# Fourier synthesis moved into the prologue of the spiking stage, row block by row block; mixed orders stored through ScalarE's queue

## The chip, the cores and the metric

One Trainium2 (trn2) chip, one core. The metric is the device time of one execution in microseconds. The kernel before has a median of 1368.16 us over three runs (1367.49 to 1375.95). The profile is of one execution that took 1366.96 us.

## What is computed

The input `x` is [8, 32, 64, 128] (batch, H, W, C). Four residual stages follow one another:

```python
x = x + _L0_conv_ref(_ln_c(x), w1r, w1i, w2r, w2i)        # spectral convolution
t = t + _L0_ffn_ref(_ln_t(t))                            # integer shift on one-hot windows of each token
x = x + _L1_conv_ref(_ln_c(x), lin_w, lin_b, bn_*)       # spiking attention over 4 x 8 time steps and heads
t = t + _L1_ffn_ref(_ln_t(t), Wg, bg, W1, b1, W2, b2)    # 8 experts, the 2 best of each token
```

The change lies in the first stage and at the start of the third:

```python
xf    = rfft(x) * (sqrt(2 pi) / NLON)                    # Fourier analysis
x_ft  = einsum('lmj,bcjm->bclm', P_ANA, xf)              # Legendre analysis
top   = einsum('bixy,ioxy->boxy', x_ft[:, :, :M1, :M2], w1)   # mixing with complex weights
bot   = einsum('bixy,ioxy->boxy', x_ft[:, :, -M1:, :M2], w2)
g     = einsum('lmj,bclm->bcjm', P_SYN, out_ft) / sqrt(2 pi)  # Legendre synthesis
out   = irfft(g, n=NLON) * NLON                          # Fourier synthesis, added to x
```

## The kernel before

All of `x` stays in SBUF as `x_sb`: 128 partitions, 128 tiles (batch b by row pair), each with 128 channels and an 8-word payload. The work is laid out in blocks of program (`nc.Block`). In a block each engine runs its own list of instructions in the written order, synchronised by semaphores, and all five engines (SP too) meet at its end before the next one starts. The order within an engine is that of the code. The blocks are:

1. *Analysis* (line 246): SP loads `x` and the Legendre table `pana`, then the first four of eight chunks of mixing weights into the four slots of `wc` (`load_w`, line 211; a chunk is four DMAs of 512 KB). The coefficients go to DRAM.
2. *Mixing* (line 399), eight chunks `n`. ACT loads `coefc`, the coefficients of the chunk; DVE and ACT build `sblk` from it (`blocks`); PE does two halves of 32 matmuls into `ps_m` (line 504); DVE copies the first half to `mo` (`evacuated`, line 436), ACT the second (line 479). `mo` has two slots, so DVE and ACT wait in chunk n for the stores of chunk n - 2 (`s_mw`). On SP, for each chunk: wait for the matmuls of chunk n, load the weights of chunk n + 4, wait for both halves of `mo`, store them to the DRAM tensor `mixed` by two DMAs (lines 402 to 411).
3. *Synthesis* (line 545). SP loads the tables `psyn` (2 MB) and `einv`, reads `mixed` back as `gin` by 16 DMAs, and fills the DRAM tensor `slots` with zero rows by four DMAs of 2652 KB (line 559); no other engine waits for those here. PE does 32 Legendre matmuls into two banks `ps_g` (line 573), and ACT and DVE take turns to empty them into `h_sb` (line 542), laid out batch by batch. Then for each of the eight batches: POOL copies the batch to `hc` (line 627), PE turns eight tiles (line 586), ACT copies them to `hT` (line 616), PE multiplies them by `einv` into `ps_y` (line 594), and DVE adds the result to `x_sb` (line 642).
4. *Weights* of the spiking stage (line 678): SP loads `lw` and five parameter vectors `par`. DVE, with one POOL instruction, scales them (`bpart`, line 711), PE does eight transposes (lines 721, 723), and DVE makes `wqkv`, `bias` and `wo`.
5. *Opcodes and spikes* (line 1320). Its *prologue* prepares row block 0 (two tiles of each batch): `statistics` (line 874) on DVE, `deviation` on POOL, `u_rows` and `x_rows` (lines 1232, 1242) on ACT, `ffn_flags`, `ffn_value`, `ffn_shift`, `ffn_add` and `z_statistics` on DVE, `deviation_2` on POOL, `z_rows` (line 1252) on ACT, `turn` (line 1130) on PE, `major` (line 1262) on ACT. Then nine passes `i` over eight steps `b` follow: each step begins with `project` (PE), `sign_projected` (ACT, the tile `sig_q`), `projected` (DVE), and the functions `beside` and `behind` say what else stands in a step. SP loads constants and, in 14 DMAs, the expert weights into `routing.raw` and `routing.last` (lines 1333 to 1344).
6. *Experts* (line 1621), 156 tiles, bound by PE.

The wait that limits a step of the grid in stage 3, and the wait that stands at the end of the store's loop on SP:

```python
pe.wait_ge(s_hT, b * 2 + g + 3)      # grid(g): turned tiles copied by ACT
pe.wait_ge(s_yfree, b * 2 + g + 1)   # grid(g): bank added by DVE
for k in range(2):
    sp.wait_ge(s_mw[k], STORED * NCH // 2)
```

## Time and profile before

| what | value |
|---|---|
| runs, median (range) | 1368.16 us (1367.49 to 1375.95) |
| profiled execution, its own time | 1366.96 us |
| its span, first to last instruction | 1364.5 us |
| mean granted clock of TensorE | 0.835 |
| busy: PE, PEld, DVE, ACT, POOL | 993.5, 845.5, 857.8, 655.1, 573.4 us |
| mixing, from the first matmul to the next block | 104.67 to 203.19 |
| synthesis | 203.19 to 283.73 |
| weights, and prologue up to the first sign | 283.73 to 345.76 |
| moved by DMA | 93.08 MB |

PE is TensorE's matmuls, PEld its weight loads, DVE VectorE, ACT ScalarE, POOL GpSimd, SP the engine that only issues DMAs. "L504" is line 504 of the kernel before. In a timeline row the number behind the start is the length, from the first to the last of the instructions merged in it; the bracket says how long the engine stood idle before it and what ended that. For SP the length is the time that issuing took. The span's idle shares are means over stages that are limited by different things, so times are read stage by stage.

### The profile page before, as it was taken

What the parts mean: (1) busy time and instruction counts of PE and PEld (TensorE: products, weight loads), DVE (VectorE), ACT (ScalarE), POOL (GpSimd) and SP (SyncE); (2) the same over time, 40 slices, a digit from 0 to 9 for tenths busy, and PEclk for the clock granted to TensorE, in tenths of its full rate; (3) what the DMA queues carried; (4) which work ended last, traced back from release to release, by engine and by line L of the source; (5) the groups of instructions that cost most, each with busy time, mean ns of one, the idle gap of its engine ahead of it and who ended that gap; (6) DMA issues with size and microseconds to landing.
All of it is one profiled execution on the core that took longest, in us unless ns stands there. A gap on an engine that the chain in (4) does not pass through costs nothing. (4 is left out here: it accounts for less than half of the span.)

```text
span 1364.5 us, 23969 instructions
## 1 busy us (share of the span) xinstructions
PE 993.5 (73%) x6628; PEld 845.5 (62%) x6629; DVE 857.8 (63%) x2741; ACT 655.1 (48%) x1400; POOL 573.4 (42%) x739
## 2 busy tenths in 40 slices
PE   7937665931577767676776754129999999999997
PEld 6827663721355556565565543028888888888886
DVE  6715432454557889889878454616666666666675
ACT  3427532207385887777865342114444444444443
POOL 3310000212022257566655477645555555555554
PEclk9978887875777888797867655559999999999999
DMA  9998949910001001000000000011111111111110
GB/s 277 201 236 157 210 104 261 240 43 20 19 20 49 20 19 41 15 24 23 11 26 15 28 25 27 21 51 45 42 43 46 48 48 48 45 47 48 46 37 1
DMA packets 122841, 93.08 MB, mean 68 GB/s; under 512 B 10760, under 2 KB 111476, under 8 KB 122001
## 3 DMA queue, kind: packets, MB, share of 16 engines
q1 hardware_dynamic: 103121, 66.48, 21.6%
q0 software_dynamic: 9088, 17.33, 3.9%
q10 hardware_dynamic: 10560, 8.39, 2.3%
q8 instruction: 35, 0.57, 0.2%
q14 instruction: 37, 0.30, 0.1%
HBM read 55.61 MB, written 38.39 MB: 69 GB/s over the span
## 5 line engine op out<-in xcount | busy, mean ns | idle before, releaser
L1663 POOL DMA_INDIRECT out_dram<-res,index x156 | 155.8, 999 | 217.7 <-DVE res L1746 192.4
L1793 ACT ACTIVATE sil<-ps_h 128x512 f32<-128x512 f32 x156 | 93.1, 597 | 254.6 <-PE ps_h L1845 254.6
L1711 DVE TENSOR_TENSOR act_rows<-ps_h,sil 128x512 f32<-128x512 f32 x156 | 108.0, 692 | 132.9 <-ACT sil L1793 132.8
L1864 PE MATMUL ps_y<-r_raw,aT 128*128 x1248 | 164.9, 275 | 0.0
L153 POOL DMA_INDIRECT slots<-x_sb,r_pos x128 | 130.9, 1023 | 54.0 <-issue 33.0
L1864 PEld LDWEIGHTS ps_y<-r_raw,aT 128*128 128x128 f32 x1248 | 151.7, 192 | 0.1
L1843 PE MATMUL ps_h<-wp,uTh 128*128 x312 | 137.5, 441 | 1.9 <-DVE uTl L1705 1.6
L1844 PE MATMUL ps_h<-wp,uTh 128*128 x312 | 124.4, 399 | 0.0
L1845 PE MATMUL ps_h<-wp,uTl 128*128 x312 | 122.8, 394 | 0.0
L1070 PE MATMUL ps_q<-wqkv,zT 128*128 128x256 f32 x256 | 114.5, 540 | 0.0
L1182 POOL TENSOR_TENSOR x_sb<-x_sb,sy 128x256 f32<-128x256 f32 x64 | 43.9, 687 | 145.6 <-ACT sy L1318 145.4
L1070 PE MATMUL ps_q<-zT,wqkv 128*128 128x128 f32 x256 | 72.6, 377 | 42.4 <-DVE ps_q L1038 24.0
L504 PE MATMUL ps_m<-wc,sblk 128*128 128x128 f32 x512 | 68.8, 304 | 39.9 <-DVE mo L442 22.6
L1296 ACT ACTIVATE sig_q<-ps_q,under_one 128x768 bf16<-128x768 f32 x64 | 57.4, 897 | 82.2 <-PE ps_q L1070 82.2
L1070 PEld LDWEIGHTS ps_q<-zT,wqkv 128*128 128x128 f32 x256 | 54.6, 264 | 63.6 <-ACT zT L1266 23.2
L1853 PE MATMUL ps_a<-ident,act_rows 128*128 128x128 f32 x624 | 93.5, 272 | 0.1
L504 PEld LDWEIGHTS ps_m<-wc,sblk 128*128 128x128 f32 x512 | 67.8, 220 | 41.1 <-issue 41.1
L1799 ACT ACTIVATE aT<-ps_a 128x512 f32<-128x512 f32 x156 | 92.4, 592 | 1.0 <-PE ps_a L1853 1.0
L1853 PEld LDWEIGHTS ps_a<-ident,act_rows 128*128 128x128 f32 x624 | 77.5, 140 | 21.7 <-DVE act_rows L1711 0.6
L194 POOL TENSOR_TENSOR e_tmp<-e_tmp,minus_half 128x16 f32<-128x16 f32 x16 | 46.8, 2924 | 91.3 <-DVE e_tmp L178 91.2
L1038 DVE SCALAR_TENSOR_TENSOR ps_q<-sig_q,ps_q 128x768 f32<-128x768 bf16 x56 | 54.6, 974 | 48.6 <-ACT sig_q L1296 48.4
L627 POOL COPY hc<-h_sb 128x1024 f32 x8 | 8.3, 1040 | 163.0 <-DVE h_sb L542 140.5
(233 smaller groups left out, 2482.8 us busy)
## 6 DMA issues: line engine op xcount, KB each, us to landing
slots<-zero SPq DMA_DIRECT2D x4, 2652.0 KB, 26.2
pay<-slots SPq DMA_DIRECT2D x39, 272.0 KB, 2.8
wc<-in_L_conv_w1r SPq DMA_DIRECT2D x8, 512.0 KB, 11.4
wc<-in_L_conv_w1i SPq DMA_DIRECT2D x8, 512.0 KB, 11.8
wc<-in_L_conv_w2r SPq DMA_DIRECT2D x8, 512.0 KB, 11.7
wc<-in_L_conv_w2i SPq DMA_DIRECT2D x8, 512.0 KB, 11.7
coefficients<-c ACTq DMA_DIRECT2D x4, 1024.0 KB, 8.6
coefc<-coefficients ACTq DMA_DIRECT2D x16, 256.0 KB, 6.1
```

The lines of the kernel that those rows point to most:

```text
L153: nc.gpsimd.indirect_dma_start(slots, bass.IndirectOffsetOnAxis(at, 0), x_sb[:, tile, :], None).then_inc(self.s_sc, 16)
L504: ins = nc.tensor.matmul(ps_m[:, half, t, :], sblk[:, n % 2, l, m:m + 4].rearrange("p m f -> p (m f)"), wc[:, n % WS, :, l, m:m + 4], star ...
L1070: return nc.tensor.matmul(out, lhs, rhs, start=first, stop=True, skip_group_check=True)
L1663: nc.gpsimd.indirect_dma_start(out_rows, bass.IndirectOffsetOnAxis(at, 0), res[:, m % RES, :], None, bounds_check=TOKENS - 1, oob_is_err=F ...
L1711: nc.vector.tensor_tensor(act_rows[:, k], ps_h[:, k, :, DFF:], sil[:, k], ALU.mult).then_inc(s_act, 1)
L1793: nc.scalar.activation(sil[:, k], ps_h[:, k, :, 0:DFF], ACT.Silu).then_inc(s_sil, 1)
L1799: nc.scalar.activation(aT[:, k, :], ps_a[:, :], ACT.Copy).then_inc(s_ac, 1)
L1843: nc.tensor.matmul(dst, hi, wp[:, 0, :, col], start=True, stop=False)
L1844: nc.tensor.matmul(dst, hi, wp[:, 1, :, col], start=False, stop=False)
L1845: ins = nc.tensor.matmul(dst, lo, wp[:, 0, :, col], start=False, stop=True)
L1853: ins = nc.tensor.transpose(ps_a[:, h * P:(h + 1) * P], act_rows[:, k, h // 2, (h % 2) * P:(h % 2 + 1) * P], ident[:, :])
L1864: ins = nc.tensor.matmul(dst, aT[:, k, (2 * e + h) * P:(2 * e + h + 1) * P], raw[:, 4 + h, col], start=(h == 0), stop=(h == 1))
```

## The change

It has three parts.

*Stores.* In the mixing block the two stores of `mixed` go from SP's list to ACT's, behind ACT's half of the same chunk. SP keeps only the weight loads. Every chunk is still loaded, multiplied and stored as before.

*Blocks.* The synthesis block is dissolved. Its loads, Legendre part and zero fills join the weights in one block (`synthesis_and_weights`): on SP the weights' six loads stand between `psyn` and `einv`; on PE and DVE the weights' work stands ahead of the Legendre part. The orders `h_sb` now lie in the space of the expert weights (`routing.orders`), so the loads of `routing.raw` wait until all of them are turned.

*Grid.* The Fourier synthesis goes by row block `i` (two row pairs of all batches) instead of by batch, in the prologue of the next block: `orders_turned` and `grid` on PE, `orders_copied` on ACT, `grid_added` on DVE. POOL's copy `hc` goes, since the transposes read the orders in place. The accumulators are the two banks `ps_o` and `ps_y` in turn (two matmuls each), and the turned tiles go through `ps_kv`. PE does all eight row blocks ahead of its first `turn`; DVE and ACT have them between the steps of the prologue. `u_rows` and `x_rows` of row block 1 move from before the first sign to steps 0 to 3 of the first pass, and `major(0, 0)` stands ahead of `z_rows` 1 to 3.

In what follows the rows of each engine's list are printed for three places. On ACT, at the last chunk of the mixing; `mo` is the tile of mixed orders. Before:

```order
L485 ACTIVATE mo<-ps_m 32x2x256 [waits mixed_stored_0,m_mixed]
L485 ACTIVATE mo<-ps_m 32x2x256 x3
L485 ACTIVATE mo<-ps_m 32x2x256 [waits mixed_stored_1,m_mixed]
L485 ACTIVATE mo<-ps_m 32x2x256 x3
L399 UNCONDITIONAL_BRANCH
```

The same place now:

```order
L481 ACTIVATE mo<-ps_m 32x2x256 [waits mixed_stored_0,m_mixed]
L481 ACTIVATE mo<-ps_m 32x2x256 x3
L497 DMA mixed<-mo 128x4x128 [waits m_last_degrees_out,m_first_degrees_out]
L497 DMA mixed<-mo 128x4x128
L481 ACTIVATE mo<-ps_m 32x2x256 [waits mixed_stored_1,m_mixed]
L481 ACTIVATE mo<-ps_m 32x2x256 x3
L497 DMA mixed<-mo 128x4x128 [waits m_last_degrees_out,m_first_degrees_out]
L497 DMA mixed<-mo 128x4x128
```

The stores have come to ACT, and each waits for both halves of its chunk.

On SP, from the start of the synthesis to the end of the block. Before:

```order
L548 DMA psyn<-in_legendre_synthesis 128x4096
L549 DMA einv<-in_fourier_inverse 128x256
L555 DMA gin<-mixed 32x2048 x16
L559 DMA slots<-zero 128x39x136 [waits e_zero]
L559 DMA slots<-zero 128x39x136 x3
L545 UNCONDITIONAL_BRANCH
L679 UNCONDITIONAL_BRANCH [waits barrier_Pool_Activation_PE_DVE_SP_release]
L681 DMA lw<-in_L_conv_lin_w 128x4x128
```

Now:

```order
L572 DMA psyn<-in_legendre_synthesis 128x4096
L573 DMA lw<-in_L_conv_lin_w 128x4x128
L576 DMA par<-in_L_conv_lin_b 128x4x1
L576 DMA par<-in_L_conv_bn_g 128x4x1
L576 DMA par<-in_L_conv_bn_b 128x4x1
L576 DMA par<-in_L_conv_bn_m 128x4x1
L576 DMA par<-in_L_conv_bn_v 128x4x1
L577 DMA einv<-in_fourier_inverse 128x256
L583 DMA gin<-mixed 32x2048 x16
L587 DMA slots<-zero 128x39x136 [waits e_zero]
L587 DMA slots<-zero 128x39x136 x3
L569 UNCONDITIONAL_BRANCH
```

The block's end has come directly behind the zero fills, and the six weight loads ahead of `gin`.

On DVE, at the start of the prologue; `e_st` holds the statistics. Before:

```order
L184 BN_STATS e_st<-x_sb 128x6 x16
L172 TENSOR_TENSOR e_tmp<-e_st 128x16 [waits e_statistics_chain]
...
L1360 CAST before<-before_f 128x128 [waits e_constants]
L885 TENSOR_SCALAR fl<-u 128x16 [waits e_ffn_rows,r_constants_set]
```

Now:

```order
L839 TENSOR_TENSOR x_sb<-x_sb,ps_o 128x2x2x128 [waits c_grid]
L839 TENSOR_TENSOR x_sb<-x_sb,ps_y 128x2x2x128 [waits c_grid]
L839 TENSOR_TENSOR x_sb<-x_sb,ps_o 128x2x2x128 [waits c_grid]
L839 TENSOR_TENSOR x_sb<-x_sb,ps_y 128x2x2x128 [waits c_grid]
L185 BN_STATS e_st<-x_sb 128x6 [waits c_added]
L185 BN_STATS e_st<-x_sb 128x6 x15
...
L839 TENSOR_TENSOR x_sb<-x_sb,ps_o 128x2x2x128 [waits c_grid]
L839 TENSOR_TENSOR x_sb<-x_sb,ps_y 128x2x2x128 [waits c_grid]
L839 TENSOR_TENSOR x_sb<-x_sb,ps_o 128x2x2x128 [waits c_grid]
L839 TENSOR_TENSOR x_sb<-x_sb,ps_y 128x2x2x128 [waits c_grid]
```

Four adds of a row block now stand ahead of the statistics, and four behind them.

The diff, cut to its core (the synthesis block that goes is in the functions printed above):

```diff
-        spectral_conv(nc, t, sb, pb, sem, x_sb, ident, minus_half, x_view, slots, routing)
+        mixed = spectral_conv(nc, t, sb, pb, sem, x_sb, ident, minus_half, x_view, routing)
...
-            weights = spiking_weights(nc, t, sb, pb, sem, ident, minus_half, a, routing)
+            weights = synthesis_and_weights(nc, t, sb, pb, sem, ident, minus_half, a, mixed, slots, routing)
...
-        self.raw = sb("r_raw", [P, 6, E * C])
+        kept = sb("r_raw", [P, 10, E * C])
+        self.raw, self.last = kept[:, 0:6], kept[0:C - 1, 6:10]
+        self.orders = kept[:, 0:8].rearrange("p a f -> p (a f)").rearrange("p (b h r m) -> p b h r m", b=B, h=HP, r=2)
...
                     for n in range(NCH):
-                        k = n % 2
                         if n + WS < NCH:
                             sp.wait_ge(s_mm, n + 1)
                             load_w(sp, n + WS)
-                        sp.wait_ge(s_ed, n + 1)
-                        sp.wait_ge(s_ea, n + 1)
-                        for op in range(2):
-                            sp.dma_start(mixed[op, n * LQ:(n + 1) * LQ].rearrange("l p f -> p l f"),
-                                         mo[:, k, op].rearrange("p (l m) o -> p l (m o)", l=LQ)).then_inc(s_mw[k], 16)
...
                         evacuated(n)
+                        act.wait_ge(s_ed, n + 1)
+                        act.wait_ge(s_ea, n + 1)
+                        for op in range(2):
+                            act.dma_start(mixed[op, n * LQ:(n + 1) * LQ].rearrange("l p f -> p l f"),
+                                         mo[:, n % 2, op].rearrange("p (l m) o -> p l (m o)", l=LQ)).then_inc(s_mw[n % 2], 16)
...
+        def grid_bank(u):
+            return (ps_o if u % 2 == 0 else ps_y)[:, :]
+
+        def orders_turned(pe, i, g):
+
+            need(pe, s_chT, (i - 1) * 2 + g + 1)
+            for q in range(G):
+                ins = nc.tensor.transpose(ps_kv[:, g, q * P:(q + 1) * P],
+                                          h_sb[:, g * G + q, 2 * i:2 * i + 2].rearrange("p h r m -> p (h r m)"), ident[:, :])
+            ins.then_inc(s_ct, 1)
+
+        def orders_copied(act, i, g):
+
+            act.wait_ge(s_ct, i * 2 + g + 1)
+            need(act, s_cg, ((i - 1) * 2 + g) * 2 + 2)
+            nc.scalar.activation(hT[:, g, :], ps_kv[:, g, :], ACT.Copy).then_inc(s_chT, 1)
+
+        def grid(pe, i, g):
+
+            pe.wait_ge(s_chT, i * 2 + g + 1)
+            for h in range(2):
+                u = (i * 2 + g) * 2 + h
+                need(pe, s_ca, u - 1)
+                for q in range(2):
+                    at = (h * 2 + q) * P
+                    ins = nc.tensor.matmul(grid_bank(u)[:, q * 2 * C:(q + 1) * 2 * C], hT[:, g, at:at + P], einv[:, :],
+                                           start=True, stop=True)
+                ins.then_inc(s_cg, 1)
+
+        def grid_added(dve, i):
+
+            for n in range(4):
+                u = i * 4 + n
+                dve.wait_ge(s_cg, u + 1)
+                rows = xv[:, 2 * n:2 * n + 2, i]
+                nc.vector.tensor_tensor(rows, rows, grid_bank(u).rearrange("p (b j c) -> p b j c", b=2, j=2), ALU.add).then_inc(s_ca, 1)
...
+                sp.wait_ge(s_ct, 2 * NP2)
                 for k in range(4):
                     sp.dma_start(routing.raw[0:C - 1, k, :].rearrange("p (e f) -> p e f", e=E),
...
+                grid_added(dve, 0)
                 statistics(dve, 0)
+                grid_added(dve, 1)
...
+                grid_added(dve, 2)
+                grid_added(dve, 3)
                 ffn_flags(dve, 0)
+                grid_added(dve, 4)
                 ffn_value(dve, 0)
                 ffn_shift(dve, 0)
+                grid_added(dve, 5)
+                grid_added(dve, 6)
                 ffn_add(dve, 0)
                 z_statistics(dve, 0)
+                grid_added(dve, 7)
                 statistics(dve, 1)
...
-                u_rows(act, 0, 0, NT)
-                x_rows(act, 0, 0, NT)
-                for g in range(G):
+                for i in range(3):
+                    copied(i)
+                u_rows(act, 0, 0, 8)
+                copied(3)
+                u_rows(act, 0, 8, NT)
+                copied(4)
+                x_rows(act, 0, 0, 5)
+                copied(5)
+                x_rows(act, 0, 5, 10)
+                copied(6)
+                x_rows(act, 0, 10, NT)
+                copied(7)
+                z_rows(act, 0, 0)
+                major(act, 0, 0)
+                for g in range(1, G):
                     z_rows(act, 0, g)
-                major(act, 0, 0)
-                u_rows(act, 1, 0, NT)
-                x_rows(act, 1, 0, NT)
...
-                    if b == 0 and 2 <= n < NP2:
+                    if b == 0 and n < NP2:
                         u_rows(act, n, 0, 10)
...
+                pe.wait_ge(s_einv, 16)
+                for i in range(NP2):
+                    for g in range(2):
+                        orders_turned(pe, i, g)
+                    for g in range(2):
+                        grid(pe, i, g)
                 pe.wait_ge(s_set, 1)
                 turn(pe, 0, 0)
...
+                        if k == 0:
+                            pe.wait_ge(s_ca, 4 * NP2)
                         if k >= 0:
                             attend(pe, i - 1, b)
```

## Rows read from the trace of the kernel before

**Rows 1.** Windows by stage: length, busy us (instructions) by engine, granted clock, DMA share, GB/s.
```profile
104.67:203.19 98.52, 68.76 (x512) 67.75 (x512) 45.38 (x110) 56.37 (x116) 0.00 (x0) 0.85 0.83 161
203.19:283.73 80.54, 57.95 (x256) 46.29 (x256) 28.77 (x40) 17.07 (x24) 8.26 (x8) 0.84 0.90 215
283.73:345.76 62.03, 7.28 (x28) 5.06 (x28) 25.99 (x144) 29.43 (x81) 11.26 (x11) 0.55 0.16 36
```

**Rows 2.** Timeline of SP's queue, weight loads: start, length, line, tile, count.
```profile
43.66 2.61 SPq L214 DMA_DIRECT2D wc<-in_L_conv_w1r  x1
...
55.32 2.71 SPq L214 DMA_DIRECT2D wc<-in_L_conv_w1r  x1
...
114.39 0.56 SPq L214 DMA_DIRECT2D wc<-in_L_conv_w1r  x1
```

**Rows 3.** Windows of 4 us, columns as in rows 1.
```profile
104.00:108.00 4.00, 3.33 (x15) 3.36 (x16) 2.44 (x9) 3.04 (x8) 0.00 (x0) 0.50 0.53 129
...
172.00:176.00 4.00, 3.40 (x31) 3.21 (x29) 0.00 (x0) 0.00 (x0) 0.00 (x0) 1.00 1.17 232
176.00:180.00 4.00, 0.00 (x0) 0.00 (x0) 2.32 (x4) 2.05 (x4) 0.00 (x0) 0.72 0.44 132
...
192.00:196.00 4.00, 4.00 (x39) 4.00 (x38) 2.47 (x4) 0.30 (x1) 0.00 (x0) 1.00 0.43 133
...
264.00:268.00 4.00, 4.00 (x23) 3.41 (x21) 1.89 (x3) 0.24 (x1) 0.36 (x1) 1.00 1.06 244
...
284.00:288.00 4.00, 0.00 (x0) 0.00 (x0) 0.00 (x0) 0.00 (x0) 0.00 (x0) 0.88 0.52 68
```

**Rows 4.** Waits in 100 to 204: us in total, times, longest.
```profile
DVE mo L442 <- DMA mixed<-mo: 32.8, 4, 10.6
```

**Rows 5.** Timeline of PE in the mixing: start, length, tile, count, idle before.
```profile
166.39 9.01 PE L504 MATMUL ps_m<-wc,sblk 128*128 128x128 f32 x64 [4.07 <-DVE mo L442]
180.58 16.45 PE L504 MATMUL ps_m<-wc,sblk 128*128 128x128 f32 x128 [5.18 <-DVE mo L442]
```

**Rows 6.** Timeline of all engines, synthesis and weights.
```profile
203.19 0.34 SPq L548 DMA_DIRECT2D psyn<-in_legendre_synthesis  x1
...
212.07 44.23 SPq L559 DMA_DIRECT2D slots<-zero  x4
...
217.28 6.10 PE L573 MATMUL ps_g<-gin,psyn 128*128 128x256 f32 x16 [20.25 <-DMA gin<-mixed]
...
239.75 1.97 PE L586 MATMUL ps_t<-ident,hc 128*128 128x128 f32 x8 [2.64 <-POOL hc L627]
...
247.35 1.04 PE L586 MATMUL ps_t<-ident,hc 128*128 128x128 f32 x8
...
252.27 1.04 PE L586 MATMUL ps_t<-ident,hc 128*128 128x128 f32 x8
...
288.81 0.27 DVE L695 MEMSET bias<- 128x256 uint32 x1 [5.36 <-DMA par<-in_L_conv_bn_v]
...
294.62 1.11 PE L721 MATMUL ps_w<-ident,lw 128*128 128x128 f32 x4 [12.65 <-DVE bpart L711]
```

**Rows 7.** SP's own waits in 90 to 300: total, times, longest.
```profile
SPq L545 <- PEq L545: 27.2, 1, 27.2
```

**Rows 8.** Timeline of all engines, prologue.
```profile
299.18 3.19 DVE L184 BATCH_NORM_STATS2 e_st<-x_sb 128x6 f32<-128x128 f32 x16 [0.30 <-PEq L678]
...
303.56 2.90 POOL L194 TENSOR_TENSOR e_tmp<-e_tmp,minus_half 128x16 f32<-128x16 f32 x1 [4.31 <-DVE e_tmp L178]
...
312.42 0.17 DVE L885 TENSOR_SCALAR fl<-u 128x16 f32<-128x16 f32 x1 [7.87 <-ACT u L1237]
...
318.71 1.02 DVE L934 SCALAR_TENSOR_TENSOR x_sb<-eq,x_sb 128x128 f32<-128x128 f32 x4 [0.60 <-ACT x_sb L1247]
...
327.75 6.26 ACT L1258 ACTIVATE z<-x_sb,e_tmp 128x128 f32<-128x128 f32 x16 [9.14 <-POOL e_tmp L1225]
...
345.76 0.88 ACT L1296 ACTIVATE sig_q<-ps_q,under_one 128x768 bf16<-128x768 f32 x1
```

188 lines of the change are left out of this document (64 added, 124 removed).

## The prediction

> **What bounds the kernel now.** I read the stages first: the windows [rows 1] give mixing 98.5 us, synthesis 80.5 us, weights and prologue 62.0 us. The change touches these three and the first pass of the loop behind them. No engine fills any of them: TensorE (PE) is busy 68.8, 58.0 and 7.3 us. They are three chains, one behind the other, so the question is which wait ends last in each.
>
> In mixing a weight chunk (four 512 KB loads) on its own takes 11.7 us: such chunks are issued at 43.66 and 55.32. Chunk 4 is issued at 114.39 [rows 2]. At 172 to 176 the DMA engines are still full (share 1.17), and in the next 4 us the share falls to 0.44. A 0.5 MB `mixed` store alone takes 0.43 of 4 us, 1.7 us, and a 0.5 MB `coefc` load 0.53 of 4, 2.1 us [rows 3]. Chunks 4 to 7, four coefficient loads and five stores are 46.6 + 8.4 + 8.6 = 63.6 us, and 114.4 + 63.6 = 178.0, in the window where the share falls: the sum closes, so the stretch is bound by bytes. But VectorE (DVE) also stood 32.8 us in four waits for stores to land [rows 4], since the stores are behind the weight loads on SP. So when the bytes are through, two chunks of matmuls are still to do: PE runs both (16.45 us) from 180.58 to 197.0 [rows 5]. ScalarE (ACT) empties the last bank, and the next block starts at 203.19 [rows 6].
>
> In synthesis the `gin` loads give PE its first work 14.1 us after the block starts (217.28). The Legendre part ends at about 238.2 (PE stands 2.64 us before the first turn at 239.75, the last copy of about 1 us among it); then come eight batches, the first in 7.6 us, the others in 4.92 us each (247.35 to 252.27). Beside it SP needs until 256.3 to issue four zero fills (44.23 us) [rows 6]; DMA is full until nearly 268 [rows 3]. SP then waits 27.2 us for PE: a block ends for all engines together [rows 7]. Weights then take 15.4 us, and the prologue 46.6 us from 299.18 to the first sign at 345.76 [rows 6, 8].
>
> **The change, part by part.** Times are in the profiled execution (1366.96 us, span 1364.5).
>
> *Mixing.* Stores no longer queue behind the weight loads, and DVE's waits fall away. What is late next is the last weight chunk. Before it must land: 46.6 us of weights, 8.4 of coefficients and, now that stores keep up, six stores, 10.3: 114.4 + 65.3 = 179.7. PE has finished chunk 6 by then (its weights land some 12 us earlier), so one chunk remains instead of two. PE has stood before it: a chunk after such a wait took 9.01 us, the second of two in a row 16.45 - 9.0 = 7.4 [rows 5] (in 172 to 176 the granted clock was 1.00, 2.4 GHz, and 0.72 in the next 4 us, part at 1.2 GHz, when PE stood). It ends at 189 where it ended at 197.0: **-8 us**. On ACT the store waits for DVE's half of the same chunk, which is done before ACT's, and blocks nothing. Bounds: 0 if two streams in the engines cost what the order saves; -16 if the stores cost nothing and the last chunk is fast. I take -8, from the sum that closed.
>
> The row at 172 says full engines, whatever the order of issue. The Trainium skill, "DMA: Bandwidth & Descriptors", section "Issuing engines are not separate DMA queues", says that starting DMAs from several engines saves only the sequencer's issue time, since all share the same 16 engines. By that rule the sum would be 8 us higher; DVE's 32.8 us of waits speak for an effect of the order, so I keep it as a rival below.
>
> *Synthesis block with the weights in it.* Count from its start. The weights' six loads (0.52 of 4 us, 2.1 us [rows 3]) come behind the 2 MB table and ahead of `gin`. My estimate for their landing is 10: 5.1 us as before (283.73, idle until 288.81) and 5 more for the table. From there to the end of PE's eight transposes is 7.8 us (288.81 to 294.62 and two groups of 1 us [rows 6]), so PE is free at 17.8 and Legendre starts there, not at 14.1. It takes 20.9 us and ends at 38.7. The weights' 15.4 us are hidden by loads. But the block cannot end there: SP issued its last fill 53.1 us after the block start (212.07 + 44.23 - 203.19), and now has 2.1 us more of data ahead, so it ends at 55.5. The fills' old cover, the grid, has left the block, and 16.8 us of the gain are lost. Before, block and weights took 299.18 - 203.19 = 96.0: **-40.5 us**. Bounds: 38.7 if SP does not hold the others, 60 if fills and weights disturb each other.
>
> *Prologue with the grid in it.* The same transposes and wide matmuls come in eight rows of 4.92 us; POOL's `hc` copies go. With the slow first row that is 39.4 + 2.7 = 42.1 us. The accumulators are two banks in turn, so PE runs at most two halves (1.9 us) ahead of DVE, and what DVE does between adds holds PE. Statistics take 4.3 us (299.18 to 303.5) and hold row 1 by 2.9, as the add before them has to be done first. Flags, value and shift take 5.7 us (312.42 until 0.60 us before 318.71 [rows 8]); flags, over half, hold row 4 by 1.6, the rest row 5 by 0.9. Row 6 ends at 2.7 + 7 x 4.92 + 5.4 = 42.5. DVE adds it (0.8; its mean instruction in [rows 1] is 0.72), does `ffn_add` (1.1) and the second statistics (4.2): 48.6. ACT's `u` and `x` rows (each at most the 6.26 us of the 16 `z` rows) lie between its copies, under the grid. Then the old chain: POOL 3.5 (2.90 and two small ones), first four `z` rows 1.6, turn, copy and gaps 1.6, and twelve `z` rows 4.7 that stand ahead of the first sign: **60 us** for 46.6 before, **+13.4 us**. The last PE row waits for DVE until 48.6 too and ends at 51, under this chain. Constants queue behind what is left of the fills (268 - 256.3 = 11.7 us), land at about 12, and are wanted at 17: hidden; uncovered they would cost a few us. Bounds: 54 (no holds) to 86 (grid, then the prologue with little overlap).
>
> *First pass of the loop.* `u_rows` and `x_rows` of row block 1, at most 12.5 us of ACT, stood before the first sign and now lie behind signs 0 to 3, in four portions of 3 us and less, where ACT waits for PE and DVE in turn: +1 us, bounds 0 to +6. What took them away is in the 60. The raw weight loads start about 11 us earlier in the span, and nobody waits for them until the experts: 0. The `s_ca` wait before the first attention is met long before: 0.
>
> Sum: -8 - 40.5 + 13.4 + 1 = -34.1, and 1366.96 - 34.1 = 1332.9. The median of the runs is 1.2 us over the profiled one, which gives 1334. I say **1333.5 us**, -2.5%.
>
> **The rivals.**
> 1. *SP does not hold the block.* 16.8 us more are gained: 1317. For it: no engine is seen waiting for SP at a block's end. Against: SP waited 27.2 us for PE at the same line.
> 2. *The store move gives nothing*: 1341.5. For it: full DMA engines. Against: DVE's 32.8 us, and two chunks left at the end.
> 3. *The grid does not overlap the prologue*, 86 us instead of 60: 1359.5, within 1%. For it: PE, ACT and DVE wait for each other in each row. Against: in four of eight rows nothing but adds stands on DVE.
> 4. *The fills become the bound and the kernel is slower.* Place: the end of the synthesis block. If fills, `gin` and weights' small loads in one ring crawl, SP's 44 us of issue grow and every engine waits. From 34 us more there is no gain, from 48 us more (92 us of issue, half the rate) it is slower by over 1%, 1382. Against: even the fills' last window shows 244 GB/s and a share of 1.06 [rows 3], and nothing ahead of them is large but the table and `gin`, as before.
>
> **How the numbers follow.** The forecast has 0.62 (its own range 1326 to 1342), rival 1 0.13, rival 2 0.12, rival 3 0.10, rival 4 0.03. The range 1314 to 1347 holds the first three and leaves out rivals 3 and 4 and the outer bounds of the others, about 0.2. A measurement of this kernel can tell about 1% from no change: below 1354.5 are the forecast, rivals 1 and 2 and the half of rival 3 with part of the overlap, 0.91; within 1% 0.06; slower 0.03.
>
> **What would show it.** Right: PE waiting for the last weights before chunk 7 and the next block at about 195; the last fill's issue ending last in the block at about 250.5, the others waiting for SP; PE waiting for DVE's adds in rows 1, 4, 5 and 7; the first `sig_q` at about 311. Wrong: a block that ends before SP's last fill (rival 1), a next block at 203 (rival 2), a first sign beyond 330 (rival 3), or passes of the loop longer than before.

## The result, and the profile after

The changed kernel takes 1331.38 us in the median of five runs (1325.47 to 1350.04). The kernel before, in the same series, has 1368.16 us (1367.40 to 1383.62). The ratio is 0.974, with a 95% interval of 0.969 to 0.979: 2.6% faster. The forecast was 1333.5 us, within 1314 to 1347. The total came out about 2 us off, but the terms of the sum were off in opposite directions: mixing gained more than forecast, the other three stages less. The stages show that, not the total.

The execution whose profile came with this result was disturbed in the analysis stage, which no edit touches (the last section is about that), so the rows below are from a second profile of the same kernel, `after_again`, with a span of 1324.6 us. I cut both profiles at the same events: first mixing matmul, first DMA of the next block (`psyn`), first DMA of the block behind it (`rank`), first sign (`sig_q`), ninth sign. The table has those differences, and forecast ones beside them:

| us | before | forecast | after_again | measured change |
|---|---|---|---|---|
| until the first mixing matmul | 104.7 | 104.7 | 104.8 | +0.1 |
| mixing | 98.5 | 90.5 | 81.6 | -16.9 |
| synthesis and weights | 95.9 | 55.5 | 56.8 | -39.1 |
| prologue | 46.6 | 60 | 62.4 | +15.8 |
| first pass, eight signs | 43.2 | 44.2 | 46.4 | +3.2 |
| rest of the span | 975.5 | 975.5 | 972.6 | -2.9 |

**Windows.** These are the three stages of the changed kernel, with the columns of [rows 1]: stretch, length, busy us and instructions of PE, PEld, DVE, ACT and POOL, granted clock, DMA share, GB/s.

```profile
104.80:186.36 81.56, 64.06 (x512) 62.87 (x512) 45.39 (x110) 56.41 (x116) 0.00 (x0) 0.92 0.91 194
186.36:243.16 56.80, 20.18 (x72) 13.43 (x73) 14.54 (x39) 8.36 (x8) 1.03 (x2) 0.68 1.07 251
243.16:305.56 62.40, 50.19 (x212) 38.85 (x212) 40.65 (x145) 26.87 (x66) 9.06 (x8) 0.83 0.32 78
```

The first row answers to the first of [rows 1]. PE does the same 512 matmuls, and the DMA engines move the same bytes at 194 GB/s instead of 161. The second row shows the block as it is now: PE has 20 us of work in 57, and DMA is full (1.07). The grid has gone to the third row, where PE is now busy 50 of 62 us.

**Mixing.** The timeline of PE, for all of the stage: start, length, line, tile, count, and in brackets what ended the idle time before.

```profile
104.80 16.66 PE L505 MATMUL ps_m<-wc,sblk 128*128 128x128 f32 x128 [16.41 <-ACT sblk L472]
123.57 7.38 PE L505 MATMUL ps_m<-wc,sblk 128*128 128x128 f32 x64 [2.11 <-ACT sblk L472]
...
163.61 7.38 PE L505 MATMUL ps_m<-wc,sblk 128*128 128x128 f32 x64 [1.11 <-ACT sblk L472]
172.76 7.41 PE L505 MATMUL ps_m<-wc,sblk 128*128 128x128 f32 x64 [1.76 <-DMA wc<-in_L_conv_w2i]
```

In place of the two chunks at the end of [rows 5] (x128, behind a wait for DVE's `mo`) there is one, and it waits for the last weight load. DVE's 32.8 us of waits for stores [rows 4] are gone. The form is as forecast; the times are not. The last weights were forecast 75.0 us after the first mixing matmul (179.7), and the chunk at 9.0 us. It starts 68.0 us after it and takes 7.4. The other waits of PE in the stage are for ACT's `sblk`: ACT's list comes round every 10.0 us per chunk (its copies to `mo` start at 124.31, 134.28, 144.27 and 154.23), so ACT now sets the pace nearly as tightly as the weights do.

**Block.** The timeline of all engines in the block. SPq rows are DMA issues.

```profile
186.36 0.35 SPq L572 DMA_DIRECT2D psyn<-in_legendre_synthesis  x1
...
189.63 5.40 SPq L576 DMA_DIRECT2D par<-in_L_conv_bn_m  x1
...
196.19 7.68 SPq L583 DMA_DIRECT2D gin<-mixed  x16
197.51 0.27 DVE L599 MEMSET bias<- 128x256 uint32 x1 [18.09 <-DMA par<-in_L_conv_bn_v]
...
203.31 1.12 PE L634 MATMUL ps_w<-ident,lw 128*128 128x128 f32 x4 [23.14 <-DVE bpart L615]
203.91 38.82 SPq L587 DMA_DIRECT2D slots<-zero  x4
...
205.07 4.33 PE L645 MATMUL ps_g<-gin,psyn 128*128 128x256 f32 x12
...
224.30 1.01 DVE L566 COPY r_raw<-ps_g 128x512 f32<-128x512 f32 x1 [1.22 <-PE ps_g L645]
...
243.17 1.94 PE L811 MATMUL ps_kv<-ident,r_raw 128*128 128x128 f32 x8 [18.91 <-PEq L569]
```

The parameters have landed at 197.51, 11.1 us into the block (forecast 10), and Legendre starts 18.7 us into it (forecast 17.8). The last Legendre copy (the orders now lie in the space called `r_raw`) ends at 225.3. SP issues zero fills until 242.7. PE then does its first turn, after 18.91 us without anything of its own to wait for: `PEq L569` is the block's own line, its end. This answers to SP's wait of 27.2 us in [rows 7], with the roles exchanged.

**Prologue.** The timeline of PE at the start of the rows that it had to wait for DVE, and the one of ACT at the end:

```profile
256.56 2.05 PE L829 MATMUL ps_o<-einv,hT 128*128 128x256 f32 x4 [2.68 <-DVE x_sb L839]
...
274.79 1.10 PE L829 MATMUL ps_o<-einv,hT 128*128 128x256 f32 x4 [1.47 <-DVE x_sb L839]
...
280.81 1.10 PE L829 MATMUL ps_o<-einv,hT 128*128 128x256 f32 x4 [0.94 <-DVE x_sb L839]
...
294.60 2.04 PE L829 MATMUL ps_o<-einv,hT 128*128 128x256 f32 x4 [3.61 <-DVE x_sb L839]
...
297.52 1.65 ACT L1226 ACTIVATE z<-x_sb,e_tmp 128x128 f32<-128x128 f32 x4 [8.09 <-POOL e_tmp L1193]
300.92 4.71 ACT L1226 ACTIVATE z<-x_sb,e_tmp 128x128 f32<-128x128 f32 x12
305.54 0.88 ACT L1264 ACTIVATE sig_q<-ps_q,under_one 128x768 bf16<-128x768 f32 x1
```

They are rows 1, 4, 5 and 7 of the eight, counted from 0, and no others.

### The profile page after: what moved, and what is told of

Same layout as the page of the kernel before. It is cut to its first block and busy times, and to the rows that moved or that the text cites. A ratio compares the mean times of both kernels' runs of the same rounds, so it can differ in the third digit from the quotient of the medians.

```text
span 1348.2 us, 23795 instructions
## 1 busy us (share of the span) xinstructions
PE 1019.1 (76%) x6628; PEld 869.1 (64%) x6629; DVE 859.9 (64%) x2741; ACT 656.3 (49%) x1400; POOL 565.4 (42%) x731
## 5 line engine op out<-in xcount | busy, mean ns | idle before, releaser
L1662 POOL DMA_INDIRECT out_dram<-res,index x156 | 156.0, 1000 | 217.2 <-DVE res L1745 186.2
L505 PE MATMUL ps_m<-wc,sblk 128*128 128x128 f32 x512 | 63.5, 289 | 29.5 <-ACT sblk L472 27.7
L505 PEld LDWEIGHTS ps_m<-wc,sblk 128*128 128x128 f32 x512 | 62.3, 204 | 30.9 <-issue 28.8
L1038 PE MATMUL ps_o<-spk,kvm 128*128 128x64 bf16 x256 | 20.8, 211 | 77.9 <-DVE ps_o L1025 76.9
## 6 DMA issues: line engine op xcount, KB each, us to landing
wc<-in_L_conv_w1i SPq DMA_DIRECT2D x8, 512.0 KB, 12.7
wc<-in_L_conv_w2i SPq DMA_DIRECT2D x8, 512.0 KB, 11.9
```

Source lines behind the costliest of these rows:

```text
L505: ins = nc.tensor.matmul(ps_m[:, half, t, :], sblk[:, n % 2, l, m:m + 4].rearrange("p m f -> p (m f)"), wc[:, n % WS, :, l, m:m + 4], star ...
L1038: return nc.tensor.matmul(out, lhs, rhs, start=first, stop=True, skip_group_check=True)
L1662: nc.gpsimd.indirect_dma_start(out_rows, bass.IndirectOffsetOnAxis(at, 0), res[:, m % RES, :], None, bounds_check=TOKENS - 1, oob_is_err=F ...
```

## The experiments

Eleven runs were made, one of them the changed kernel again. Each was profiled once and timed against the kernel before on the same chip. Ratios are to the kernel before, with their 95% interval. Their totals scatter by some 1% with the analysis stage (after_again's six executions took 1324.62 to 1347.21 us), so a verdict on a stage goes by the stage's own length, cut as above:

| us | mixing | Legendre end | block | prologue | first pass | rest | span |
|---|---|---|---|---|---|---|---|
| before | 98.5 | 35.0 | 95.9 | 46.6 | 43.2 | 975.5 | 1364.5 |
| after | 82.8 | 37.9 | 56.6 | 60.1 | 46.5 | 976.5 | 1348.2 |
| after_again | 81.6 | 38.9 | 56.8 | 62.4 | 46.4 | 972.6 | 1324.6 |
| stores_sp | 97.5 | 39.2 | 57.5 | 60.4 | 45.7 | 968.2 | 1344.7 |
| stores_twice | 95.0 | 38.7 | 57.0 | 60.4 | 47.2 | 975.5 | 1361.1 |
| before_stores_act | 81.4 | 34.8 | 95.0 | 46.6 | 43.7 | 974.7 | 1354.6 |
| fills_later | 83.2 | 38.2 | 38.5 | 60.0 | 45.4 | 972.1 | 1325.5 |
| four_banks | 83.7 | 38.1 | 56.2 | 54.9 | 46.8 | 976.8 | 1321.3 |
| z_behind | 81.3 | 38.5 | 56.3 | 62.9 | 53.0 | 972.2 | 1351.2 |
| u_first | 82.6 | 38.0 | 56.7 | 72.8 | 43.2 | 973.5 | 1354.6 |
| best_a | 81.4 | 38.7 | 39.0 | 52.9 | 46.8 | 972.2 | 1305.6 |
| best_b | 81.4 | 35.2 | 35.4 | 52.9 | 46.7 | 970.0 | 1291.0 |
| weights_two | 86.9 | 38.1 | 56.3 | 60.0 | 46.5 | 973.5 | 1334.6 |

"Legendre end" is the last copy out of `ps_g`, counted from the block's start; "block" in the two kernels built as before is synthesis and weights together. What a span has over the sum of its stages is the time until the first mixing matmul, 102.9 to 126.3 us. A stage that no edit touches keeps its length within 1 to 2.5 us from kernel to kernel (the rest of the span, some 970 us, within 9), and that is what a difference has to exceed. Only best_a and best_b have totals whose intervals do not overlap that of after_again, so the other experiments speak through their stages.

### The mixing: whose 16 us?

**after_again**, the changed kernel once more, as the other end of each comparison.

> The changed kernel once more, since its profiled execution was a disturbed one: it spent 125.7 us before the first mixing matmul, where the kernel before spent 104.7. If that was the execution and not the change, the first mixing matmul is back at about 105 and the span about 21 us shorter than 1348, near 1328. If the change slows the analysis stage, it stays at 125. Mixing (first matmul to next block) 82.8 us, synthesis block 56.6, prologue to first sign 60.1 as in the first profile, all within 1 us.

Measured: 1338.62 us in the median, ratio 0.976 [0.967, 0.985]. The interval overlaps that of the first series. The first mixing matmul is back at 104.8 and the span is 1324.6, so the analysis stage was the execution's and not the change's. Mixing (81.6) and prologue (62.4) missed "all within 1 us" by a little: the first is 1.2 us shorter than in the first profile, the second 2.3 longer.

**stores_sp**: the changed kernel with the stores back on SP's list.

```diff
                         if n + WS < NCH:
                             sp.wait_ge(s_mm, n + 1)
                             load_w(sp, n + WS)
+                        sp.wait_ge(s_ed, n + 1)
+                        sp.wait_ge(s_ea, n + 1)
+                        for op in range(2):
+                            sp.dma_start(mixed[op, n * LQ:(n + 1) * LQ].rearrange("l p f -> p l f"),
+                                         mo[:, n % 2, op].rearrange("p (l m) o -> p l (m o)", l=LQ)).then_inc(s_mw[n % 2], 16)
...
-                        act.wait_ge(s_ed, n + 1)
-                        act.wait_ge(s_ea, n + 1)
-                        for op in range(2):
-                            act.dma_start(mixed[op, n * LQ:(n + 1) * LQ].rearrange("l p f -> p l f"),
-                                         mo[:, n % 2, op].rearrange("p (l m) o -> p l (m o)", l=LQ)).then_inc(s_mw[n % 2], 16)
```

> The changed kernel with only the stores of mixed orders put back on SP's queue. Theory A (the forecast: bytes bind, the order saves one chunk of matmuls): mixing 8 us longer than in the changed kernel, about 91. Theory B (stores and weight loads in two queues overlap in the DMA engines, more than one queue allows): the whole 15.7 us come back, mixing 98.5, time about 1345. Rival 2 (the store move gives nothing): no difference, 83.

Measured: 1352.45 us, ratio 0.989 [0.979, 0.998]. Mixing is 97.5 us, all of the old length but 1 us, and the other stages stay. The waits of the trace show the old row again (engine, line, what it waited for, total, times, longest):

```profile
DVE mo L443 <- DMA mixed<-mo: 32.5, 4, 10.6
```

**before_stores_act**: the same move, alone, in the kernel before. The diff is that of stores_sp read backwards, on the kernel before.

> The kernel before with only the stores moved to ScalarE's queue, the rest as it was. Forecast: 8 us faster, about 1360. Theory B: 15.7 us faster, about 1352, and mixing 82.8 as in the changed kernel. Rival 2: no difference, 1368.

Measured: 1354.97 us, ratio 0.988 [0.979, 0.997]. Mixing is 81.4 us, -17.1. So the store move is worth 16 to 17 us with or without the rest of the change, and the parts of the change do not interact here.

**stores_twice**: the changed kernel, with each chunk stored a second time, to a DRAM tensor that nobody reads.

```diff
-            STORED = 16 * 2
+            STORED = 16 * 4
...
+                        for op in range(2):
+                            act.dma_start(twice[op, n * LQ:(n + 1) * LQ].rearrange("l p f -> p l f"),
+                                         mo[:, n % 2, op].rearrange("p (l m) o -> p l (m o)", l=LQ)).then_inc(s_mw[n % 2], 16)
```

> The changed kernel with every store of mixed orders issued a second time, into a DRAM tensor that nobody reads; the output is unchanged. Theory A (bytes of all queues add up at 1.7 us for a 0.5 MB store): six more stores ahead of the last weight chunk make mixing 10 us longer, about 93. Theory B (stores in a queue of their own fill gaps of the weight loads): under 4 us longer, with more GB/s in the saturated stretch than the 237 of the changed kernel.

Measured: 1354.96 us, ratio 0.988 [0.977, 0.999]. Mixing is 95.0 us, 13.4 more than in after_again. The number is theory A's, but the trace shows another cause: the weights were not late. PE starts chunk 7 at 205.62, 70.2 us after SP issued chunk 4's weights at 135.41 (58.4 us in after_again), and what it waits for is ACT:

```profile
205.62 7.38 PE L510 MATMUL ps_m<-wc,sblk 128*128 128x128 f32 x64 [1.45 <-ACT sblk L474]
```

The last weights had landed by 194.1. This table has, for each kernel, the stretch from the first load of chunk 4 to the landing of the last load of chunk 7, and what all queues moved in it:

| | issued | landed | us | MB | DMA share | GB/s |
|---|---|---|---|---|---|---|
| before | 114.39 | 176.1 | 61.7 | 12.7 | 1.15 | 205 |
| stores_sp | 124.62 | 186.2 | 61.6 | 12.8 | 1.15 | 207 |
| after_again | 114.34 | 172.7 | 58.4 | 13.6 | 1.13 | 234 |
| before_stores_act | 122.28 | 180.9 | 58.6 | 13.7 | 1.14 | 234 |
| stores_twice | 135.41 | 194.1 | 58.7 | 15.2 | 1.13 | 258 |

With 4.6 MB of stores beside them instead of 3.1, the weights took 0.3 us longer. What the doubled stores cost is time on ACT, which issues them between its copies and the next `sblk`. These are ACT's waits with nothing but its own issues in them, first in stores_twice, then in after_again:

```profile
ACT sblk L472 <- issue: 18.8, 6, 4.0
ACT sblk L470 <- issue: 6.9, 6, 1.3
```

They differ by 11.9 us, and chunk 7 starts 11.8 us later. So theory B is right about the transfers and wrong about the stage, whose length ACT's list sets here: its round takes up to 12.9 us per chunk instead of 10.

The rate of the saturated stretch shows in windows of 15 us. The kernel before (columns as above):

```profile
120.00:135.00 15.00, 8.89 (x78) 8.54 (x76) 6.76 (x18) 12.15 (x26) 0.00 (x0) 0.95 1.18 212
135.00:150.00 15.00, 9.54 (x64) 9.38 (x64) 4.30 (x14) 5.67 (x14) 0.00 (x0) 0.83 1.16 215
150.00:165.00 15.00, 9.53 (x64) 9.37 (x64) 7.71 (x19) 9.09 (x19) 0.00 (x0) 0.77 1.18 208
```

And the same stretch of after_again, whose mixing begins within 0.2 us of it:

```profile
120.00:135.00 15.00, 10.31 (x85) 9.98 (x84) 9.14 (x25) 11.69 (x26) 0.00 (x0) 0.94 1.17 238
135.00:150.00 15.00, 13.86 (x117) 13.70 (x117) 10.69 (x26) 11.55 (x24) 0.00 (x0) 0.95 1.16 247
150.00:165.00 15.00, 11.29 (x84) 10.96 (x84) 8.82 (x25) 12.50 (x27) 0.00 (x0) 0.89 1.16 246
```

The share is the same, 1.16 to 1.18, in both: by it the engines were full before, and are full now. The last column rose from 212 to 244 GB/s, and the table has 258 in stores_twice. A full share is not a full rate, and that is what the forecast's byte sum took it for.

**weights_two**: of each chunk's four loads from the fifth chunk on, two are issued by SP and two by GpSimd (POOL), with a semaphore of their own. It asks whether more queues for the loads gain more.

```diff
-                            load_w(sp, n + WS)
+                            load_w(sp, n + WS, range(2))
...
                     nc.gpsimd.memset(sblk[:, 1], 0.0).then_inc(s_zero, 1)
+                    for n in range(NCH - WS):
+                        pool.wait_ge(s_mm, n + 1)
+                        load_w(pool, n + WS, range(2, 4), s_p)
...
-                        pe.wait_ge(s_w[n % WS], n // WS * 64 + 64)
+                        pe.wait_ge(s_w[n % WS], n // WS * 32 + 64)
+                        need(pe, s_p[n % WS], n // WS * 32)
```

> The changed kernel, but of each mixing chunk's weights from the fifth on two of the four transfers are issued by GpSimd and two by SP; bytes and waits are the same. It asks where the mixing stage's missing 8 us went (forecast 90.5, measured 81.6 to 82.8). If more queues at once fill gaps that one queue leaves in the engines (loads alone ran at 181 to 185 GB/s, loads with stores on another queue at 232 to 256), a third queue fills more of them: mixing 72 to 78, GB/s of the stretch above 240 from the fifth chunk's issue on. If the 16 us came from SP no longer issuing stores ahead of loads (order within the queue, not number of queues), two queues for the loads change nothing: mixing 81 to 83. If GpSimd's own queue costs more per transfer, it is longer: 85 or more.

Measured: 1335.55 us, ratio 0.973 [0.966, 0.980], and mixing of 86.9 us, 4 to 5 longer. The first two expectations missed. The third has the number right, but not the cause. PE's timeline at the end, and DVE's waits in the stage:

```profile
163.44 7.38 PE L509 MATMUL ps_m<-wc,sblk 128*128 128x128 f32 x64 [0.75 <-ACT sblk L476]
174.62 17.43 PE L509 MATMUL ps_m<-wc,sblk 128*128 128x128 f32 x128 [3.79 <-DVE mo L442]
```

```profile
DVE mo L442 <- DMA mixed<-mo: 18.2, 3, 8.6
```

PE waits for no weights. It could not gain much by them either: in the changed kernel only 1.76 us of its waits in this stage were for weights, and ACT's list takes 10.0 us per chunk, so mixing of 72 to 78 us was out of reach of any rate of the loads. The stores land later (10.0 us after their issue in the median, 18.4 at most; 8.2 and 10.0 in after_again), DVE waits for them again, and as in the kernel before, two chunks are left at the end. Here the third queue for the loads took service from the stores, and what came late decided, not the rate alone.

### The block: is it held by SP?

**fills_later**: the four zero fills go to the next block, behind its constants.

```diff
-                sp.wait_ge(routing.s_zero, 2)
-                part = SLOT_TILES // 4
-                for n in range(4):
-                    sp.dma_start(slots.rearrange("(q p) c -> p q c", p=P)[:, n * part:(n + 1) * part, :],
-                                 routing.zero[:, :].unsqueeze(1).broadcast_to([P, part, XW])).then_inc(routing.s_clear, 16)
...
+                sp.wait_ge(routing.s_zero, 2)
+                part = SLOT_TILES // 4
+                for n in range(4):
+                    sp.dma_start(slots.rearrange("(q p) c -> p q c", p=P)[:, n * part:(n + 1) * part, :],
+                                 routing.zero[:, :].unsqueeze(1).broadcast_to([P, part, XW])).then_inc(routing.s_clear, 16)
                 sp.wait_ge(s_ct, 2 * NP2)
```

> The changed kernel with only the four zero fills moved on SP from the end of the synthesis block to the next block, behind the constants and ahead of the expert weights. Theory of the forecast (the block ends when SP has issued its last fill): the block ends with the Legendre part at about 38.5 us instead of 56.6, time 18 us less, about 1311. Rival 1 (SP does not hold the others, something else fills the gap from 246 to 265): the block stays at 56 us and the time at 1329. A third way: the fills now run beside the grid and cost it something, gain 10 to 15.

Measured: 1324.76 us, ratio 0.965 [0.957, 0.973]. The block is 38.5 us, 18.3 shorter than in after_again, and ends 0.3 us behind the last Legendre copy. PE's row of waits:

```profile
PE ps_kv L806 <- PEq L569: 1.4, 1, 1.4
```

It was 18.91 us. The fills are issued within the prologue, and that stays at 60.0 us. The total missed the 1311 us of the expectation: the profiled execution stood 126.3 us in the analysis stage, 21 more than after_again. Rival 1 of the forecast (SP does not hold the block) is refuted by both kernels: one shows engines standing for SP's issue, the other what it costs.

### The prologue

**four_banks**: the grid's accumulators go round four PSUM banks instead of two, so PE may run four halves ahead of DVE's adds.

```diff
-            return (ps_o if u % 2 == 0 else ps_y)[:, :]
+            return (ps_o[:, :], ps_y[:, :], ps_q[:, 0], ps_q[:, 1])[u % 4]
...
-                need(pe, s_ca, u - 1)
+                need(pe, s_ca, u - 3)
...
+            if k == 0:
+                pe.wait_ge(s_ca, 4 * NP2)
```

> The changed kernel with the grid's accumulators in four banks in turn (the two banks of ps_q join ps_o and ps_y) instead of two. Forecast's theory (PE is held in rows 1, 4 and 5 by 5.4 us in sum, because DVE does other work between adds and PE is only two halves ahead): prologue 5 us shorter, first sign at 55 us from the block's start instead of 60.1, waits of PE for DVE's adds in those rows gone. Rival (DVE's own chain is the limit, PE only waits beside it): prologue stays within 1 us of 60.

Measured: 1325.28 us, ratio 0.974 [0.966, 0.982], prologue 54.9 us, 5.2 less than in the first profile of the changed kernel and 7.5 less than in the second. PE's waits for DVE's adds are gone from the trace. So the three holds inside the grid, 2.9 + 1.6 + 0.9 = 5.4 us in the forecast and 2.7 + 1.5 + 0.9 = 5.1 in the trace, stood on the path in full. The 2.3 us by which the two profiles of the changed kernel differ are no part of that.

**u_first**: `u_rows` and `x_rows` of row block 1 stand before the first sign again, where the kernel before has them.

```diff
                 for g in range(1, G):
                     z_rows(act, 0, g)
+                u_rows(act, 1, 0, NT)
+                x_rows(act, 1, 0, NT)
...
-                    if b == 0 and n < NP2:
+                    if b == 0 and 2 <= n < NP2:
```

(and the same condition for b = 1 to 3)

> The changed kernel with u_rows and x_rows of row block 1 put back ahead of the first sign, as in the kernel before. Forecast's term (their place in steps 0 to 3 costs 1 us, ahead of the sign they would cost 11.5 less what the first projection hides): 8 to 11 us slower than the changed kernel, first sign at 71, first pass 43.2 us again instead of 46.5. If their place makes no difference: within 1 us.

Measured: 1354.83 us, ratio 0.984 [0.974, 0.994]. The prologue is 72.8 us, 10.4 longer than in after_again and 12.7 longer than in after, and the first pass is 43.2 us, exactly as before. The rows cost 11.45 us where they stand in front:

```profile
326.50 5.19 ACT L1205 ACTIVATE u<-x_sb,e_tmp 128x48 f32<-128x48 f32 x16 [1.20 <-POOL e_tmp L1184]
331.73 6.26 ACT L1215 ACTIVATE x_sb<-x_sb,e_tmp 128x128 f32<-128x128 f32 x16
337.89 0.88 ACT L1264 ACTIVATE sig_q<-ps_q,under_one 128x768 bf16<-128x768 f32 x1
```

and 3.2 us in the steps of the first pass. That is the answer to the term of +1 for this edit.

**z_behind**, a miss: twelve of the sixteen `z` rows go behind the first three signs, in the hope of a first sign 4.7 us earlier.

```diff
-                for g in range(1, G):
-                    z_rows(act, 0, g)
...
+                        if i == 0 and b < 3:
+                            z_rows(act, 0, b + 1)
```

> The changed kernel with the twelve z rows of groups 1 to 3 moved from ahead of the first sign to behind signs 0, 1 and 2 of the first pass. If ScalarE's 4.7 us stand on the path to the first sign: first sign 2 to 3 us earlier (it then waits for PE's projection), and the first pass up to 3 us longer since ScalarE is full there too: gain 0 to 3 us. If ScalarE has room in those steps the gain stays at 3.

Measured: 1347.08 us, ratio 0.982 [0.974, 0.991]. The prologue does not get shorter (62.9 us), and the first pass is 53.0 us, 6.6 longer. PE turns each group of `z` for a step still ahead, and now waits for it (rows of PE's timeline, one for each of the three groups that were moved):

```profile
328.42 1.12 PE L1105 MATMUL ps_turn<-ident,z 128*128 128x128 f32 x4 [2.52 <-ACT z L1226]
335.72 1.12 PE L1105 MATMUL ps_turn<-ident,z 128*128 128x128 f32 x4 [2.77 <-ACT z L1226]
343.43 0.66 PE L1105 MATMUL ps_turn<-ident,z 128*128 128x128 f32 x4 [3.18 <-ACT z L1226]
```

The first sign needs PE's projection, and that was on its way while ACT did the twelve rows. With the rows gone, ACT stands idle for most of their 4.71 us:

```profile
325.94 0.90 ACT L1264 ACTIVATE sig_q<-ps_q,under_one 128x768 bf16<-128x768 f32 x1 [3.87 <-PE ps_q L1038]
```

Where they stood they cost less than 1 us.

### A version that beats both

**best_a** is fills_later and four_banks together, with no further edit.

> The changed kernel with the two edits that paid by their stages put together: zero fills issued in the next block, behind its constants, and the first grid's accumulators in four PSUM banks. If the two gains are independent, the stages add up: mixing 81.6, block 38.5 (fills out of it), prologue 55 (from 60.1 to 62.4), first pass 46 to 47, rest unchanged; that is 18 + 5 to 7 us below the changed kernel's own stages, a total near 1310 us (ratio 0.957 to the kernel before). The rival: with the fills in the prologue, SP's queue and the 16 engines are busy until about 33 us after the block's start, and the rows that now leave two PSUM banks earlier meet the fills; then the prologue stays at 58 to 60 and the total at 1316.

Measured: 1307.41 us, ratio 0.950 [0.939, 0.961]. Block 39.0, prologue 52.9 us. The gains add up, and the rival (the fills in the prologue meet the faster rows) is refuted: the prologue is 2 us shorter than in four_banks, which is within what it varies by, and not longer than there.

**best_b** is best_a with the weights' six loads moved to the end of the mixing block, into tiles of their own.

```diff
+        self.lw = sb("lw", [P, 4, C])
+        self.par = sb("par", [P, 5, 4])
...
                             load_w(sp, n + WS)
+                    sp.dma_start(routing.lw[:, :, :], t["L1_conv_lin_w"].rearrange("i d c -> d i c")).then_inc(routing.s_load, 16)
+                    for n, name in enumerate(("lin_b", "bn_g", "bn_b", "bn_m", "bn_v")):
+                        with nc.allow_non_contiguous_dma(reason="512 parameters, once"):
+                            sp.dma_start(routing.par[:, n, :], t[f"L1_conv_{name}"].rearrange("i d -> d i")).then_inc(routing.s_load, 16)
...
-        lw = sb("lw", [P, 4, C], at=a)
-        par = sb("par", [P, 5, 4], at=a)
+        lw, par = routing.lw, routing.par
```

> best_a, and the longitude block's Linear weights and its five parameter vectors are loaded at the end of the mixing stage's load queue, into tiles of their own. If the 5 to 6 us by which the Legendre stage's end is later in the changed kernel than its own PE work asks (the five vectors' transfers, 5 us each in the queue, ahead of the grid's input) are the cause, the Legendre stage ends 35 us or less after the block's start instead of 38 to 39, and the block is 3 to 5 us shorter: 34 to 35.5. The rival: the vectors' small packets are only waited for elsewhere (in the mixing stage, behind the last chunk's weights), then mixing grows by what the block loses, 3 to 5 us, and the total stays that of best_a.

Measured: 1297.06 us, ratio 0.946 [0.938, 0.954]. The interval overlaps that of best_a, so the totals alone do not tell the two apart; the stage does. Legendre ends at 35.2 us and the block at 35.4, 3.6 less than in best_a, and mixing is unchanged at 81.4. The expectation had 5 us of queue for each of the five vectors; in the changed kernel one issue took 5.40 us and the others 0.50 to 1.06. What was late is no longer the parameters but `gin` (waits of PE and DVE in the block; the first row is DVE waiting for the mixing block to end):

```profile
DVE bias L596 <- PEq L403: 7.1, 1, 7.1
PE ps_g L642 <- DMA gin<-mixed: 6.7, 1, 6.7
```

The three stages in windows:

```profile
104.40:185.84 81.44, 64.19 (x512) 63.06 (x512) 45.42 (x111) 56.40 (x116) 0.00 (x0) 0.92 0.89 197
185.84:221.29 35.45, 20.40 (x72) 13.68 (x72) 14.59 (x39) 8.31 (x8) 1.01 (x1) 0.73 0.71 182
221.29:274.17 52.88, 42.02 (x212) 34.75 (x212) 39.70 (x145) 26.57 (x65) 10.26 (x10) 0.94 0.99 232
```

The fills' DMA work has moved to the third row (share 0.99, where after_again has 0.32), beside a PE that is busy four fifths of the time, and the prologue is no longer for it (52.9 us, 54.9 in four_banks). These three stages take 169.8 us, where the changed kernel has 200.8 and the kernel before 241.1. The mixing holds a second test of its pace: the last weights landed 54.8 us after chunk 4's issue, 3.6 sooner than in after_again, and the stage did not get shorter, since PE waited for ACT's `sblk` instead (1.60 us before chunk 7).

## Why the prediction was right or wrong

**Mixing, -8: mis-sized, it is -16.9.** The mechanism was right: the stores' place on SP was the cause, DVE's waits went, and one chunk is left at the end instead of two. The step that failed is "before it must land: 46.6 us of weights, 8.4 of coefficients and six stores, 10.3". The sum of 65.3 us took the share of 1.17 for the limit of the engines and added loads and stores as if one had to wait for the other. It measured 58.4 us, 7 less. About 2 us of that were wrong before the change: the sum closed at 178.0, but the weights had landed at 176.1, 61.7 us after the issue, and the SP queue had moved 2.1 MB of stores by then, which is four chunks and not five. Another 1.7 are the sixth store, which cost the loads nothing, and 3.3 are the higher rate with the stores in ACT's queue. The remaining 1.6 us are the last chunk itself, 7.4 us instead of 9.0: PE had stood only 1.76 us before it, and the granted clock of 165 to 180 is 1.00, of the 15 us before it 0.89. The far bound of -16 was given for just these two things, stores that cost nothing and a fast last chunk; the measured value is just beyond it. Had the weights landed as late as in the kernel before, 71.4 us after the first matmul and not 67.9, the stage would be 3.5 us longer. So by this estimate most of the gain, some 13 us, is the order in SP's list, as forecast but larger, and some 3.5 us are the second queue. What the forecast did not see at all is that ACT, with its 10.0 us per chunk, is as long as the weights now: in best_b they came 3.6 us sooner for nothing. I had one hint and did not weigh it: the sum closed for one queue, and I then used it for two. Rival 2, the store move gives nothing, rested on the same rows, and it is refuted by stores_sp and before_stores_act. The Trainium skill, "DMA: Bandwidth & Descriptors", section "Issuing engines are not separate DMA queues", says that starting DMAs from several engines saves only issue time. The order's part does not speak against that; the rise of the rate does (205 to 234 GB/s over the stretch by the queue of the stores alone, and 258 with the stores doubled, at the same share), and there the measurement decides. The run with a third queue bounds the lesson: it gained nothing.

**Block, -40.5: right, -39.1.** Parameters at 11.1 instead of 10 us, Legendre from 18.7 instead of 17.8, its end at 38.9 instead of 38.7, the block's end at 56.8 instead of 55.5, held by SP's last fill. The 16.8 us "lost" by it are there and were won back by fills_later (18.3). The fills' issue is shorter than before (38.8 for 44.23 us) but begins 8.7 us later (17.5 for 8.9), since the six loads of the weights now stand ahead, one of them with 5.4 us of issue. The forecast had 2.1 us for them, by their bytes; what they cost is issue. The later start (+8.7) and the shorter issue (-5.4) make +3.3 together, so the sum came out close by two errors that nearly cancel (and its 53.1 + 2.1 is 55.2, not 55.5).

**Prologue, +13.4: right in its parts, +13.5 and +15.8 in the two profiles.** The holds were forecast at rows 1, 4, 5 and the last, at 2.9, 1.6 and 0.9 us; they are at those four, at 2.7, 1.5 and 0.9. DVE frees the last row at 294.6, 51.4 us after the start, for 48.6 forecast. The 2.3 us between the two profiles arise in row blocks 0 and 1 (0.9 and 1.4 us), where PE ran more of its matmuls at the lower clock in after_again (granted 0.58 in the 5 us from 245, against 0.81 in the 5 us from 267 of the first profile). Row 1 of the first profile, after its wait, is

```profile
277.56 1.10 PE L829 MATMUL ps_o<-einv,hT 128*128 128x256 f32 x4 [2.68 <-DVE x_sb L839]
```

against 2.05 us at 256.56 above for the same four matmuls, after the same 2.68 us of standing: the clock was 1.00 there and 0.50 here. The forecast had a slow first row only.

**First pass, +1: within its bounds (0 to +6), but three times too small, +3.2.** "Four portions of 3 us and less, where ACT waits for PE and DVE in turn" holds only in part: the first four steps grew by 1.6 us (19.2 to 20.8), and the next four, in which nothing was moved, by another 1.6 (24.0 to 25.6). Prologue and first pass together take 116.0 us in u_first and 106.6 or 108.8 in the two profiles of the changed kernel, so moving these rows is worth 7 to 9 us.

**The cases.** Rivals 1 and 2 fell as told. Rival 3 (no overlap, 86 us) fell: 50 us of PE, 41 of DVE and 27 of ACT lie in 62.4. Rival 4 (fills crawl) fell: 38.8 us of issue, under the 44.2 of before. The sum was -34.1; the same four stages give -37.0, and the two spans differ by 39.9, of which 2.9 lie in the rest of the span, within its scatter. The measured total of the first series is -35 by its ratio, and it carries the scatter of the analysis stage as well. So the closeness of 1331.4 to 1333.5 is better than the terms deserved: -8.9 in the mixing stands against +1.4, +2.4 and +2.2 in the other three.

## What to carry to other kernels

A DMA share of one says that the engines have work, not that they move what they can: compare the GB/s of windows before a byte sum is used as a floor, and where stores stand behind loads in one queue, try them in another one before counting bytes. Ask then whose list has become longer: the doubled stores cost the transfers 0.3 us and ACT's list 11.9. A stage length that fits a theory's number does not show its cause; the wait before the last chunk does. All engines meet at the end of a block, SP too, so long DMA issues that nobody waits for belong behind the block's last useful wait or in a block whose length something else sets. When work is moved off a chain, ask of each instruction left whether it is under somebody else's wait: the `z` rows cost less than 1 us in front of the sign and 6.6 us behind it, and the `u` and `x` rows the other way round.
